# Constants on ScalarE's queue, an early average for the first group norm, and half chunks at the start of the product

## What is computed

```python
x = x + _L0_conv_ref(_gn(x), ...)
# in _L0_conv_ref, on the group-normed x:
qkv = einsum('bchw,oc->bohw', x, w_qkv) + b_qkv
qkv = qkv.reshape(b, 3 * c, hs, DS, ws, DS).max(axis=(3, 5))
qkv = depthwise 3x3 conv(qkv, w_dw) + b_dw
# channel attention with four top-k softmaxes, gelu, upsampling, projection
```

## Time and profile before

| | us |
|---|---|
| median of 3 runs | 2866.84 (2865.65 to 2867.16) |
| the profiled execution | 2862.79 |
| its span in the profile | 2861.0 |
| TensorE busy | 2578.9 (90%), 17291 products |
| VectorE busy | 2522.8 (88%) |
| ScalarE busy | 1478.1 (52%) |
| GpSimd busy | 73.7 (3%) |

### The profile page before, as it was taken

One profiled execution on the slowest core, in us unless ns is written; L12 is line 12 of the kernel. 1 busy time (PEld: TensorE's weight loads), 2 busy tenths in 40 slices (PEclk: granted clock), 3 DMA queues, 4 the chain that ended last, 5 costly groups with the idle time before them and its releaser, 6 DMA issues. The chain is left out here.

```text
span 2861.0 us, 51217 instructions
## 1 busy us (share of the span) xinstructions
PE 2578.9 (90%) x17291; PEld 1860.0 (65%) x17291; DVE 2522.8 (88%) x3511; ACT 1478.1 (52%) x1925; POOL 73.7 (3%) x144
## 2 busy tenths in 40 slices
PE   0039999999999999999998699998599999999998
PEld 0026666666666666666665466665499999999997
DVE  6968999999999999999999689989688888888884
ACT  0043355555555554554422367777566666666663
POOL 0010000000000000000000100000000000000000
PEclk9999999999999999999999799999799999999999
DMA  8955112332323223223000599998999999999996
GB/s 329 417 211 174 62 34 85 107 91 69 99 85 101 80 83 110 86 70 105 18 17 9 201 343 342 350 344 297 233 285 289 289 290 289 295 299 292 287 289 184
DMA packets 363929, 546.38 MB, mean 191 GB/s; under 512 B 146048, under 2 KB 257408, under 8 KB 363776
## 3 DMA queue, kind: packets, MB, share of 16 engines
q1 hardware_dynamic: 334160, 466.53, 52.5%
q10 hardware_dynamic: 29616, 77.86, 8.2%
HBM read 363.88 MB, written 180.44 MB: 190 GB/s over the span
## 5 line engine op out<-in xcount | busy, mean ns | idle before, releaser
L774 PE MATMUL qk_qb<-qk_xhi,whi 128*128 128x384 f16 x2592 | 846.1, 326 | 19.4 <-DVE qk_xlo L670 14.3
L774 PE MATMUL qk_qb<-qk_xlo,whi 128*128 128x384 f16 x2592 | 846.0, 326 | 0.0
L774 PE MATMUL qk_qb<-qk_xhi,wlo 128*128 128x384 f16 x2592 | 846.0, 326 | 0.0
L691 DVE SCALAR_TENSOR_TENSOR qk_dw<-qk_pool,qk_wd,qk_dw 128x768 f32<-128x768 f32 (+2 forms) x864 | 837.1, 1009 | 2.1 <-ACT qk_dw L543 2.0
L678 DVE TENSOR_REDUCE qk_pool<-qk_qb 128x192 f32<-128x768 f32 x432 | 411.7, 953 | 65.2 <-PE qk_qb L774 48.6
L1656 PE MATMUL cv_cb<-cv_hi,cv_toep 128*128 128x288 f16 x1536 | 347.0, 286 | 30.3 <-DVE cv_lo_last L1588 24.9
L774 PEld LDWEIGHTS qk_qb<-qk_xhi,whi 128*128 128x128 f16 x2592 | 253.9, 98 | 182.5 <-DVE qk_xlo L670 16.6
L774 PEld LDWEIGHTS qk_qb<-qk_xhi,wlo 128*128 128x128 f16 x2592 | 253.9, 98 | 168.1 <-issue 0.8
L774 PEld LDWEIGHTS qk_qb<-qk_xlo,whi 128*128 128x128 f16 x2592 | 253.9, 98 | 162.7 <-issue 0.8
L1662 PE MATMUL cv_cb<-cv_hi_next,cv_toep 128*128 128x288 f16 x1536 | 346.1, 287 | 0.0
L1531 ACT ACTIVATE cv_res<-cv_cb,cv_cst 128x288 f32<-128x288 f32 x384 | 187.6, 502 | 298.4 <-PE cv_cb L1662 235.1
(11 more groups left out here) (180 smaller groups left out, 3442.4 us busy)
## 6 DMA issues: line engine op xcount, KB each, us to landing
cv_toep<-toeplitz_scratch SPq DMA_DIRECT2D x384, 256.0 KB, 6.2
patch_scratch<-pr_turned SPq DMA_DIRECT2D x75, 832.0 KB, 9.3
cv_raw<-patch_scratch SPq DMA_DIRECT2D x240, 260.0 KB, 6.2
st_x<-in_x SPq DMA_DIRECT2D x24, 2304.0 KB, 17.1
qk_xf<-in_x SPq DMA_DIRECT2D x72, 768.0 KB, 4.2
pr_xb<-in_x SPq DMA_DIRECT2D x24, 2304.0 KB, 9.9
out<-cv_rows ACTq DMA_DIRECT2D x72, 768.0 KB, 7.1
toeplitz_scratch<-qk_band ACTq DMA_DIRECT2D x48, 416.0 KB, 2.6
```

The costliest lines, as they stand in the source:

```text
L691: V.scalar_tensor_tensor(acc, pool[:, o, r + y:r + y + n, x:x + PW], wd[:, o, k:k + 1], acc, ALU.mult, ALU.add).then_inc(taps_done, 1)
L774: ins = nc.tensor.matmul(qbank[s % NQB][:, h, 0:2 * W], w[:, b, o * P:(o + 1) * P], x[:, par, j // 2, b, at_row:at_row + 2 * W], start=n = ...
```

## The change

The 24 loads of constants move from SyncE's to ScalarE's queue, ahead of ScalarE's own work. The group norm's own block goes. VectorE sums the means of the first 20 chunks; TensorE turns them into a group average `base` while the last four are read; after the last chunk VectorE sums deviations from `base` and their squares over all 288 half records of each channel, and TensorE averages both columns at once, at the start of stage_qkv, followed by 20 products whose result is overwritten. The group's mean and variance come from these, and ScalarE's root gives 1/`sx` directly. Products with parts of `member` that hold only zeros are left out, seven of nine remaining. Chunk 1 is read at once into `second`, which is the memory of `dw`. Chunks 0 and 1 are normed, rounded and subtracted in halves of 768 pixels, four pieces n of three blocks, six of the twelve norms on VectorE; slots 0 to 3 wait each for its own piece. GpSimd starts after `prep`, and from the zeroing of `dw` on after the last early low.

```diff
-def group_affine(nc, tag, stats, member, mean, rstd):
...
@@ -192,12 +131,6 @@
...
             for i in range(XBUFS):
                 sp.dma_start(xs[:, i], src[:, :, i * CHUNK:(i + 1) * CHUNK]).then_inc(x_in[i], 16)
-            sp.dma_start(wst[:, :, :], wT.rearrange("(b p) n -> p b n", p=P)).then_inc(w_in, 16)
-            sp.dma_start(kern[:, :, :, :], w_large.rearrange("(b p) o y x -> p b (o y) x", p=P)).then_inc(c_in, 16)
-            sp.dma_start(ws[:, :, :, :], w_small.rearrange("(b p) o y x -> p b (o y) x", p=P)).then_inc(c_in, 16)
-            for n, a in enumerate(norms):
-                sp.dma_start(bn[:, n, :], a.rearrange("(b p) -> p b", p=P), allow_slow_non_contiguous=True).then_inc(c_in, 16)
-            ahead.constants(sp)
             with sp.Fori(1, STEPS // XBUFS) as r:
                 for i in range(XBUFS):
...
         @block.scalar
         def _(act):
+            act.dma_start(wst[:, :, :], wT.rearrange("(b p) n -> p b n", p=P)).then_inc(w_in, 16)
+            act.dma_start(kern[:, :, :, :], w_large.rearrange("(b p) o y x -> p b (o y) x", p=P)).then_inc(c_in, 16)
+            act.dma_start(ws[:, :, :, :], w_small.rearrange("(b p) o y x -> p b (o y) x", p=P)).then_inc(c_in, 16)
+            for n, a in enumerate(norms):
+                act.dma_start(bn[:, n, :], a.rearrange("(b p) -> p b", p=P), allow_slow_non_contiguous=True).then_inc(c_in, 16)
+            ahead.constants(act)
             act.wait_ge(w_in, 16)
             nc.scalar.activation(whi[:, :, :], wst[:, :, :], ACT.Copy, scale=SCALE).then_inc(whi_ready, 1)
...
-            with dve.Fori(1, STEPS // XBUFS) as r:
+            with dve.Fori(1, ROUNDS - 1) as r:
                 statistics(r)
+            records = stats[:, :, :, :].rearrange("p b n (two s) -> p b (n two) s", two=2)
+            dve.wait_ge(x_used, (ROUNDS - 1) * XBUFS)
+            V.tensor_reduce(sums[:, :], records[:, :, 0:KNOWN, 1], AX.X, ALU.add).then_inc(sums_ready, 1)
+            statistics(ROUNDS - 1)
+            dve.wait_ge(guess_done, 1)
+            chained(V.tensor_scalar(base[:, :], guess[:, 0:CB], 1.0 / KNOWN, None, ALU.mult))
+            dve.wait_ge(x_used, STEPS)
+            chained(V.tensor_tensor(dev[:, 0], records[:, :, :, 1],
+                                    base[:, :].unsqueeze(2).broadcast_to([P, CB, 2 * STEPS * REC]), ALU.subtract))
+            chained(V.tensor_tensor(dev[:, 1], dev[:, 0], dev[:, 0], ALU.mult))
+            V.tensor_reduce(part[:, 0], records[:, :, :, 2], AX.X, ALU.add)
+            V.tensor_reduce(cols[:, :, 0], dev[:, 0], AX.X, ALU.add)
+            chained(V.tensor_reduce(part[:, 1], dev[:, 1], AX.X, ALU.add))
+            V.scalar_tensor_tensor(cols[:, :, 1], part[:, 0], 2.0 / 512, part[:, 1], ALU.mult, ALU.add)
...
+        @block.tensor
+        def _(pe):
+            pe.wait_ge(made, 3 + 2 * CB)
+            pe.wait_ge(sums_ready, 1)
...
+                for b in near:
+                    ins = nc.tensor.matmul(guess[:, o:o + 1], member[:, b, o * P:(o + 1) * P], sums[:, b:b + 1],
+                                           start=b == near[0], stop=b == near[-1])
+            ins.then_inc(guess_done, 1)
...
+    def load_into(sp, buf, t, b, done):
+        sp.dma_start(buf, src[:, b, t * CHUNK:(t + 1) * CHUNK]).then_inc(done, 16)
...
+    HALVES = CHUNK // 2
...
+        averages = tbank[0]
+        second = dw[:, :, :].rearrange("p r n -> p (r n)")[:, 0:CB * CHUNK].rearrange("p (b n) -> p b n", b=CB)
...
+        PIECES = [(h, k) for h in range(HALF) for k in range(2)]
+        BY_DVE = ((0, 1), (1, 1), (1, 2), (2, 1), (3, 1), (3, 2))
+        BY_ACT = tuple((n, b) for n in range(2 * HALF) for b in range(CB) if (n, b) not in BY_DVE)
...
+        def early(n, b):
+            h, k = PIECES[n]
+            return (xf[:, b] if h == 0 else second[:, b])[:, k * HALVES:(k + 1) * HALVES]
...
 
             for b in range(CB):
-                load(1, b)
+                start.load_into(sp, second[:, b], 1, b, x2_in[b])
             for b in range(CB):
-                load(2, b)
+                sp.wait_ge(lo_half, b + 1)
+                sp.wait_ge(lo_ready, b + 1)
+                start.load(sp, 2, b)
             sp.wait_ge(blank_made, 1)
...
 
-                act.wait_ge(x_in[b], t * 16 + 16)
+                act.wait_ge(x_in[b], t * 16)
...
+            def early_high(n, b):
+                h, k = PIECES[n]
+                early_normed(act, n, b)
+                nc.scalar.activation(xhi[:, 0, h, b, k * HALVES:(k + 1) * HALVES], early(n, b),
+                                     ACT.Copy).then_inc(hi_half if k == 0 else hi_ready, 1)
...
+            act.wait_ge(var_ready, 1)
+            nc.scalar.activation(root[:, :], var[:, :], ACT.Sqrt, bias=eps[:, :], scale=UNSCALE).then_inc(root_ready, 1)
             act.wait_ge(prep, 2)
             act.wait_ge(c_in, 16 * (3 + 2 + len(TOPK)))
-            for h in range(HALF):
+            for n in range(2 * HALF):
                 for b in range(CB):
-                    norm(h, b)
-                    high(h, 0, h, b)
+                    if (n, b) in BY_ACT:
+                        early_norm(n, b)
+                for b in range(CB):
+                    early_high(n, b)
             for b in range(CB):
                 norm(HALF, b)
             act.wait_ge(zeroed, 4)
...
+            gp.wait_ge(prep, 2)
             G.memset(pool[:, :, :, 0:PW + 2:PW + 1], 0.0).then_inc(zeroed, 1)
             G.memset(pool[:, :, 0:2, 1:1 + PW], 0.0).then_inc(zeroed, 1)
             G.memset(pool[:, :, UR + 2, 1:1 + PW], 0.0).then_inc(zeroed, 1)
+            gp.wait_ge(lo_half, HALF * CB)
+            gp.wait_ge(lo_ready, HALF * CB)
             G.memset(dw[:, :, 0:PW], 0.0).then_inc(zeroed, 1)
             G.memset(padw[:, :, :, :, :], 0.0).then_inc(pad_made, 1)
...
-            V.tensor_scalar(sx[:, :], rstd[:, :], SCALE, None, ALU.mult).then_inc(prep, 1)
+            V.memset(eps[:, :], 1e-5 * UNSCALE).then_inc(eps_ready, 1)
+            dve.wait_ge(avg_done, 1)
+            V.tensor_scalar(off[:, :], averages[:, 0:2 * CB:2], 1.0 / RECORDS, None, ALU.mult).then_inc(link, 1)
+            dve.wait_ge(link, 1)
+            V.tensor_tensor(sq[:, :], off[:, :], off[:, :], ALU.mult).then_inc(link, 1)
+            dve.wait_ge(link, 2)
+            V.scalar_tensor_tensor(var[:, :], averages[:, 1:2 * CB:2], 1.0 / RECORDS, sq[:, :],
+                                   ALU.mult, ALU.subtract).then_inc(var_ready, 1)
+            V.tensor_tensor(mean[:, :], base[:, :], off[:, :], ALU.add).then_inc(link, 1)
+            dve.wait_ge(root_ready, 1)
+            V.reciprocal(sx[:, :], root[:, :]).then_inc(prep, 1)
             dve.wait_ge(prep, 1)
+            dve.wait_ge(link, 3)
             V.scalar_tensor_tensor(bx[:, :], mean[:, :], -1.0, sx[:, :], ALU.mult, ALU.mult).then_inc(prep, 1)
+            dve.wait_ge(prep, 2)
...
+            def early_low(n, b):
+                h, k = PIECES[n]
+                early_normed(dve, n, b)
+                if k == 0:
+                    dve.wait_ge(hi_half, h * CB + b + 1)
+                else:
+                    dve.wait_ge(hi_ready, h * CB + b + 1)
+                window = slice(k * HALVES, (k + 1) * HALVES)
+                V.tensor_tensor(xlo[:, 0, h, b, window], early(n, b), xhi[:, 0, h, b, window],
+                                ALU.subtract).then_inc(lo_half if k == 0 else lo_ready, 1)
...
-            for h in range(HALF):
+            early_norm(0, 1)
+            early_norm(1, 1)
+            early_norm(1, 2)
+            for b in range(CB):
+                early_low(0, b)
+            early_norm(2, 1)
+            for b in range(CB):
+                early_low(1, b)
+            early_norm(3, 1)
+            early_norm(3, 2)
+            for n in range(2, 2 * HALF):
                 for b in range(CB):
-                    low(h, 0, h, b)
+                    early_low(n, b)
...
+            WARM = 20
+            for o in range(CB):
+                near = [b for b in range(CB) if abs(b - o) <= 1]
+                for b in near:
+                    ins = nc.tensor.matmul(averages[:, 2 * o:2 * o + 2], member[:, b, o * P:(o + 1) * P], cols[:, b, :],
+                                           start=b == near[0], stop=b == near[-1])
+            ins.then_inc(avg_done, 1)
+            for n in range(WARM):
+                nc.tensor.matmul(qbank[1][:, 0, 0:2 * W], whi[:, 0, 0:P], whi[:, 0, 0:2 * W],
+                                 start=n == 0, stop=n == WARM - 1)
...
                     if live:
-                        if s < JPO and s % 2 == 0:
+                        if at(t, 0) and s < JPO and s % 2 == 0:
+                            pe.wait_ge(lo_half, s // 2 * CB + CB)
+                        elif at(t, 0) and s < JPO:
+                            pe.wait_ge(lo_ready, s // 2 * CB + CB)
+                        elif s < JPO and s % 2 == 0:
                             pe.wait_ge(lo_ready, (t * 2 + s // 2) * CB + CB)
```

(17 more changed lines are left out.)

81 lines of the change are left out of this document (24 added, 57 removed).

## The result

The changed kernel takes **2876.80 us** (median of 7 runs, 2875.14 to 2877.89), the kernel before 2866.84 (7 runs, 2865.20 to 2867.16): ratio 1.0037, 95% interval 1.0026 to 1.0048, slower by 10.0 us. Forecast were 2881.6 and a range of 2851 to 2889. The profiled execution of the changed kernel took 2876.8 (span 2875.1).

The account below looks back on a forecast made before the run. TensorE sets the pace from its first product, so early changes count by when it runs without a gap; +22.8 - 4.3 + 0.5 - 10.4 + 4.5 + 1.7 = +14.8 on 2866.84 gives 2881.6 us, range 2851 to 2889.

Parts of the forecast that it names:

- The constants: Statistics: small loads on ScalarE's queue take turns with x, delaying weight split and VectorE's restart to 72.3: +22.8 us.
- Rival (a): Statistics: ScalarE's constants pass quickly, in groups or as small HBM loads, so no stall; 2851.9 us; chance 22%.
- VectorE's pace: Statistics after restart: 20 chunks at VectorE's 5.46 instead of the DMA's 5.67, -4.3 us; sum of known means +0.5.
- The group norm: Tail from last chunk to ScalarE's first norm: 8.2 us with handovers for 18.6, -10.4 us.
- The early average: Group norm: TensorE makes it beside the last four chunks, with 20 us to spare, so the next step doesn't wait.
- the warm-up products: Start of stage_qkv: 20 products, some 6 us behind the averages, over before the first piece is ready; cost nothing.
- Halves and chunk 3: Start of the product: halves' 4.1 us gain lost; GpSimd's late zeroing delays stores and chunk 3's load, +4.5 us.
- the clock: TensorE after idling 8 us for chunk 3: clock at half for a while, +1.7 us.
- Rival (b): The constants' stall comes, but blank stores don't hold TensorE up: -4.1+1.7 in place of +6.2, 2873 us; chance 12%.

Follow-up runs that it names:

- e1: The changed kernel with the 24 loads of constants back on SyncE's queue, behind chunks 0 to 3: 2860.19 us, ratio 0.9976 to the kernel before.
- e2: The kernel before with only the 24 loads of constants moved to ScalarE's queue: 2884.48 us, ratio 1.0067.
- e4: The changed kernel with GpSimd's zeroing of `blank` and `late` ahead of its wait for the early lows: 2869.89 us, ratio 1.0009 to the kernel before.
- e8: The kernel before with only the new group norm (constants on SyncE, whole chunks, no warm-up products): 2856.20 us, ratio 0.9958.
- e10: The changed kernel with the edits of e1 and e4 together: 2856.05 us, ratio 0.9956 to the kernel before.
- e5: The changed kernel with 26 more products, never read, behind slot 1 to keep TensorE busy ahead of slot 2: 2889.88 us, ratio 1.0079 to the kernel before.
- e7: The changed kernel with the edits of e4 and e5 together: 2881.37 us, ratio 1.0060 to the kernel before.
- e9: The changed kernel with ScalarE's weight split behind its load, roots between norm loads and next stage's constants, VectorE's folding after chunk 16: 2852.06 us, ratio 0.9945 to before.

## Why the prediction was right, and where not

**The constants.** The chain was as forecast: turns packet by packet on loads too, ScalarE free at 61.01 (forecast 60), the split behind it, restart 73.48 for 49.52: **+24.0** for +22.8. e1 and e2 show that this is the queue's alone. The Trainium skill (DMA: Bandwidth & Descriptors, Queues, rings and completion order) has a DMA engine drain a packet of typically 9 to 17 descriptors before it turns to the other queue. This trace doesn't agree: the two queues pass 2038 and 2037, never more than four of one in a row. Rival (a), which the prediction drew from groups of small loads against single rows, is out. (With groups on both queues the stall would have been the same, so (a) needed the single rows as well.) The step missed nothing of size: ScalarE had issued eleven loads by 48.9, with some five of them outstanding, and the other 13 took 12.1 us.

**VectorE's pace.** The 20 later chunks and the sums of known means took 181.04 - 73.48 = 107.56 us, where before 163.13 - 49.52 = 113.61: **-6.1** for -4.3 + 0.5. The term was mis-sized: `bn_stats` runs back to back at 5.36 a chunk (21.44 for 36 instructions / 4), not 5.46.

**The group norm.** From 181.04 to N 8.3 us, before 18.6: **-10.3** for -10.4. The early average was ready, and the warm-up products cost nothing. N is later by 24.0 - 6.1 - 10.3 = 7.6, as the table has it.

**Halves and chunk 3.** This is the term that was furthest off. Forecast +4.5 and +1.7; M - N rose by **2.4**. The place was right: the load of chunk 3 behind GpSimd's zeroing, a stall in slot 19 and a lower clock after it. But chunk 3 came at N+69.3, not N+73.2, against N+68.7 before: GpSimd needed 7.3 us from the zeroing of `dw` to `late`, not 9.4 (each cast of `kern` took 0.33 us, where two of the three had taken 0.95 and 1.86), so the stores began at N+24.0 instead of N+25.4; and from there to the chunk took 45.2 us, not 47.8. So TensorE stalled for 2.77 us and not 8, and its stall ended at N+77.0 (before N+76.3): the term was worth +0.7, the clock the forecast +1.7. The halves' 4 us (slot 2 at N+17.5 for N+21.4) were real and lost in the wait for chunk 3, as e4 shows: 95.15 - 90.05 = 5.1 us, about the halves' 3.9 and the old stall's 0.96. (The kernel before kept its clock in slot 2; e2 and e8, which start that stage in the same way, did not, and have 95.53 and 95.72. So some 0.5 of the 2.4 us may be chance.) Half a clock in slot 2, which I had not forecast, was hidden in that same wait; in e10, with the wait gone, it comes out as 92.86 - 90.05 = 2.8.

**The sum.** 24.0 - 6.1 - 10.3 + 2.4 = +10.0, measured +10.0; forecast +14.8. What is over is 3.8 of the halves and 2.3 of the pace, less 1.2 of the constants and 0.1 of the group norm. The parts are read from the two profiled executions up to M. As wholes those two differ by 14.0 us, 3.6 of it behind the last maximum (1304.8 and 1308.4), so that the parts meet the difference of the medians to 0.1 us is partly luck. The 4.05 us between the profiled execution and the median of before was carried over as if it were the kernel's; the changed kernel's profiled execution lies on its median. This did no harm, since the sum was added to the median.

Rival (b), 2873, has chunk 3 nearly right (+0.7) but no stall there and the halves' gain kept; its number is 3.8 us too low, mine 4.8 too high. The time alone doesn't decide between the two. The stall in slot 19 does: it is there, 2.77 us, and the halves' gain is lost in it.

What stays open: why e5's and e7's loops wait at their edges. Code that runs once stands ahead of an unchanged loop; the trace shows the new waits as TensorE's own issue and nothing that ends them. Whether the place of the loop's code, the length of what stands ahead or something else decides wasn't tried.

## What to carry to other kernels

Moving small loads to a second queue frees the first but gave them no bandwidth here: beside the stream of x each small packet waited for one row, so what a load cost was its packets times the other queue's packet time (24 x 0.236 = 5.7 us), whatever its bytes. The engine that issues such loads starts nothing else while an issue holds it; so on that engine put each instruction that someone waits for right behind the load that it needs, and move the consumer's wait as far back as it can go (e9: the same loads, 24.7 us less). When a step is held back, ask what else its engine does in order behind it; two memsets in the wrong place hid the whole gain of the halves (M - N 97.57 with them there, 90.05 in e4).
